# W2's 16-bit halves made in sweeps 0 and 1 and kept in memory, and block one-hots by one narrow 16-bit operation per pair

## The chip, the cores and the metric

One core of a Trainium2 chip. The time is the device time of one execution in microseconds (us), the median of several runs.

## What is computed

T=4096 tokens of D=256 features, a dense 4096x4096 adjacency of zeros and ones, E=8 experts.

```python
h = layernorm(x);   x = x + (adj @ (h @ W0 + b0)) / deg          # deg: column sums of adj
h = layernorm(x)
p = softmax(h @ Wg + bg); top 2 of 8, renormalised -> combine
x = x + sum_e combine_e * (gelu(h @ W1[e] + b1[e]) @ W2[e] + b2[e])
h = layernorm(x);   A = adj + I;  x = x + relu((d^-1/2 A d^-1/2 h) @ WL.T + bL)
x = x + a table step on the layernormed row (argmax of three groups of 16, a shift, two one-hots)
```

Products run on pairs of 16-bit numbers: a value v is kept as hi = fp16(v) and lo = fp16(v - hi), and three of the four products are summed.

## The kernel before, in words

The program has three blocks. A block begins only when all engines have ended the block before.

**Block 1, sweeps.** The first graph layer runs as NS=4 sweeps of 1024 columns. In a sweep SP loads 32 tiles of the adjacency (512 KB each) into a ring of 8; TensorE takes 8 products of 512 columns per tile (L914), ScalarE sums each tile for the degrees (add_degree, L802). A tile's buffer is free when both have used it. In sweep 0 the rows of x are normalised on the way: VectorE (rows, L484), then ScalarE casts the high half (high_row, L798; four rows ahead, then 4/3 rows per tile), then GpSimd takes the low half (split_row, L392). From tile 20 on TensorE transposes three rows per tile and multiplies them by the gate weights; each transposed row goes through take_transposed on VectorE (L545), with two buffers. At tile 21 it transposes W0, for which the row of b0 must have landed (L958); GpSimd issues that load behind its last split_row (L404), then two stores of zero rows, and waits for them (L408). Sweep 1 begins when VectorE has taken the gate sums (xg_taken, L559). In sweeps 1 to 3 the products of the sweep before leave by rows_out (L926), a row per tile from tile 4 on (from 20 in sweep 3).

**The weights.** The experts' weights are 32 units of 128x1024: u 0 to 15 of W1, 16 to 31 of W2. In memory of the core they take 16-bit halves for the whole of block 2. W1's 16 units are split in the sweeps at the tiles named by UNIT_AT (L277): SP loads a unit into one of two buffers (L311), ScalarE casts the high half behind add_degree (L810), VectorE makes the low half (split_unit, L492) at places written out by hand in its order (L573 to L595). W2's 16 units come behind sweep 3, during the last rows and the routing: SP loads them as f32 (load_middle_unit, L340; four late ones at L365), ScalarE makes the high half and a scaled copy (high_middle, L874), GpSimd subtracts (split_middle, L438); the four late ones are cast by ScalarE at the end of the block (L907) and subtracted by VectorE at the start of block 2 (split_late, L1235). Second-layer products wait for w2_parts (L1162).

**Late rows and routing.** GpSimd loads x a second time in pairs of tiles (load_x_again, L410) for the residual sums; the rows of tiles 16 to 31 are normalised on ScalarE (L825) and low halves made on GpSimd (L416) between the units of W2. VectorE ranks the tokens (L686 to L741) and then builds, in 16 batches of HOTS=4 pairs, one-hots of row and block; TensorE multiplies them (L1019) into the table of tokens. The block one-hot is two operations per batch, over 4x80 elements in f32 through a bank of PSUM (L756, L757).

**Block 2** gathers rows per expert slot (L1057), runs two layers on TensorE and adds the results to x_rows. **Block 3** is the second graph layer and the table step. The diff does not touch block 3.

Of the kernel before, what the change touches and what calls it, by code (L numbers as in the profile page):

```python
# [3 lines left out]
P = 128  # L4
# [67 lines left out]
def program(nc, x, adjT, W0, b0, Wg, bg, W1, b1t, W2, b2, WL, bL, identity, upper, out):  # L72

    ln_rows = nc.dram_tensor("ln_rows", [T + P, ROW], F32, kind="Internal").ap()
# [78 lines left out]

    stage = [Region(X_AT + 16384 + k * 4096, end)(f"stage{k}", [P, 1024], F32) for k in range(MIDDLE_RING)]
    late_stage = [Region(W_AT - 16384 + k * 4096, W_AT)(f"late_stage{k}", [P, 1024], F32) for k in range(UNITS - LATE_UNIT0)]
# [88 lines left out]
    same_blk = [pb[k][:, 0:HOTS * BLOCKS].rearrange("p (q b) -> p q b", b=BLOCKS) for k in (4, 3)]  # L244
# [36 lines left out]
    assert len(UNIT_AT) == W2_UNIT0 and NS == 4 and RING == G  # L281

    def unit_out(u, h):
        return w1_v[:, u, h, :, :]

    def unit_in(t):
        return unit_f[t][:, :].rearrange("p (h f) -> p h f", h=2)

    def middle_stage(u):
        return stage[(u - W2_UNIT0) % MIDDLE_RING]  # L290

# [15 lines left out]
    with nc.Block() as block:  # L307

        @block.sync
        def _(sp):  # L310
            def load_unit(u):  # L311
                sp.wait_ge(sem("unit_lo"), u + 1)
                sp.dma_start(unit_f[u % 2][:, :], W1_unit[u]).then_inc(sem(f"unit_loaded{u % 2}"), 16)
# [26 lines left out]
            def load_middle_unit(u):  # L340
                k = u - W2_UNIT0
                if k >= MIDDLE_RING:
                    sp.wait_ge(sem("middle_lo"), k - MIDDLE_RING + 1)
                sp.dma_start(middle_stage(u)[:, :].rearrange("p (f d) -> p f d", d=D), W2_u[k]
                             ).then_inc(sem(f"middle_loaded{k % MIDDLE_RING}"), 16)

            for k in range(4):
                sp.wait_ge(sem("adj_used"), 3 * NT + 29 + k + RING)
                sp.wait_ge(sem("deg_ready"), 3 * NT + 29 + k + RING)
                load_middle_unit(W2_UNIT0 + k)  # L350
            for g in range(2):
                store_x1(g)
            for k in range(4, 6):
                load_middle_unit(W2_UNIT0 + k)
            store_x1(2)
            for k in range(6, 8):
                load_middle_unit(W2_UNIT0 + k)
            store_rows(2)
            store_x1(3)
            for k in range(8, 10):  # L360
                load_middle_unit(W2_UNIT0 + k)
            store_rows(3)
            for k in range(2):
                sp.wait_ge(sem(f"early_stored{k}"), 16 * (NT // 8))
            for k in range(UNITS - LATE_UNIT0):  # L365
                sp.dma_start(late_stage[k][:, :].rearrange("p (f d) -> p f d", d=D), W2_u[LATE_UNIT0 - W2_UNIT0 + k]
                             ).then_inc(sem("late_loaded"), 16)
            for u in range(W2_UNIT0 + 10, LATE_UNIT0):
                load_middle_unit(u)
# [4 lines left out]
            sp.wait_ge(sem("late_stored"), 16 * 2)  # L374
# [3 lines left out]
        def _(pool):  # L378
# [17 lines left out]

            pool.sem_inc(sem("hid_lo_ready"), 2)
# [10 lines left out]
            pool.wait_ge(sem("spare_zeroed"), 32)  # L408

# [16 lines left out]
            pool.wait_ge(sem("unit_lo"), W2_UNIT0 + 2)  # L426
# [11 lines left out]
            def split_middle(u):  # L438
                pool.wait_ge(sem("middle_hi"), 2 * (u - W2_UNIT0) + 2)
                pool.tensor_tensor(experts[:, u, 1, :], middle_stage(u)[:, :], experts[:, u, 0, :], ALU.subtract  # L440
                                   ).then_inc(sem("middle_lo"), 1)

            for k in range(4):
                split_middle(W2_UNIT0 + k)
            for n in range(2 * G, 3 * G):
                low_row(n)
            for k in range(4, 6):
                split_middle(W2_UNIT0 + k)
            for n in range(3 * G, NT):
                low_row(n)  # L450
            for u in range(W2_UNIT0 + 6, LATE_UNIT0):
                split_middle(u)
# [4 lines left out]
        def _(v):  # L457
            v.sem_inc(sem("unit_lo"), 2)
# [114 lines left out]
            split_unit(0)  # L573
            split_unit(1)
            for n in range(NT):
# [8 lines left out]
            split_unit(3)  # L584
            take_numbers()

            for s in (1, 2):
                low_sums(s - 1)
                u = UNIT_AT[s, 4]
                split_unit(u)  # L590
                for k in range(OT):
                    take_rows((s - 1) * OT + k)
                    if k % 2:
                        split_unit(u + 1 + k // 2)
                split_unit(u + 5)  # L595
# [10 lines left out]
            def x_pair(n):  # L606
# [9 lines left out]
            def add_late_mean(n, bank):  # L616
                x_pair(n)
# [3 lines left out]
                v.scalar_tensor_tensor(out=agg[:, n, :], in0=bank[:, 0:D], scalar=rdeg[:, n:n + 1], in1=x_ring[:, n % G, :],  # L621
# [128 lines left out]
            for q in range(BATCHES):  # L750
# [5 lines left out]
                st.link(v.tensor_tensor(same_blk[i], over_pairs(count_ps[:, 0:BLOCKS]), over_columns(blk[:, k, :], n, BLOCKS), ALU.is_equal))  # L756
                v.tensor_tensor(blk_hot[i][:, :, :], same_blk[i], over_columns(val, n, BLOCKS), ALU.mult).then_inc(sem("hot_ready"), 1)  # L757
# [29 lines left out]
        def _(a):  # L787
# [13 lines left out]

            def add_degree(s, j):  # L802
# [4 lines left out]
                if (s, j) in UNIT_AT:  # L807
                    u = UNIT_AT[s, j]
                    a.wait_ge(sem(f"unit_loaded{u % 2}"), u // 2 * 16 + 16)
                    a.mul(unit_out(u, 0), unit_in(u % 2), WS).then_inc(sem("unit_hi"), 1)  # L810
# [63 lines left out]
            def high_middle(u):  # L874
                k = u - W2_UNIT0
                a.wait_ge(sem(f"middle_loaded{k % MIDDLE_RING}"), k // MIDDLE_RING * 16 + 16)
                if u == LATE_ROWS_UNIT:
# [761 lines left out]
```

## Time and profile before

| | us |
|---|---|
| median of 3 runs (lowest, highest) | 1075.37 (1074.89, 1077.36) |
| profiled execution | 1077.18 |
| its span, first to last instruction | 1075.2 |
| TensorE busy | 956.4 (89%) |
| VectorE busy | 559.4 (52%) |
| ScalarE busy | 404.4 (38%) |
| GpSimd busy | 360.0 (33%) |
| DMA | 200.00 MB, mean 186 GB/s |

An engine's share of the span is an average over stages with different limits, so the stages are read one by one below. Engines in the rows: PE is TensorE, PEld its weight loads, DVE VectorE, ACT ScalarE, POOL GpSimd, SP the engine that issues most transfers.

### The profile page before, as it was taken

To read this page: it belongs to the slowest core of one execution; us is meant where nothing else is said; L and a number is where in the kernel's file an instruction comes from. 1 tells how busy PE (TensorE), PEld (TensorE's weight loads), DVE (VectorE), ACT (ScalarE), POOL (GpSimd) and SP (SyncE) were. 2 spreads that over 40 slices of the span, in tenths; PEclk is the share of its full clock that TensorE was granted. 3 is DMA by queue.
4 is the path that set the end of the run, shared out by engine and by line. 5 is a ranking of instruction groups with operands and counts; after the bars stand their busy time and mean duration, and the time that the engine had idled before them with its cause. 6 is when DMAs were issued, how large, how long until landed. Compare 5 with 4: busy or idle time off the path is not lost. (4 is left out here: it accounts for less than half of the span.)

```text
span 1075.2 us, 22179 instructions
## 1 busy us (share of the span) xinstructions
PE 956.4 (89%) x6724; PEld 627.4 (58%) x6725; DVE 559.4 (52%) x1643; ACT 404.4 (38%) x826; POOL 360.0 (33%) x416
## 2 busy tenths in 40 slices
PE   4988999999922799999999999999819999999993
PEld 1444544444411689898989898898704454444541
DVE  6734113127598566565656565665436334161754
ACT  4863758676787233232323232323112101010111
POOL 3510000014575345454545455454425320110110
PEclk9999999999965799999999999999959999999997
DMA  9785898899786423232332323232259978876771
GB/s 346 307 293 186 287 328 319 312 345 371 257 278 183 156 41 55 45 54 45 50 50 45 54 43 56 40 55 44 46 161 393 406 254 298 291 240 189 231 254 35
DMA packets 91265, 200.00 MB, mean 186 GB/s; under 512 B 13328, under 2 KB 47120, under 8 KB 91088
## 3 DMA queue, kind: packets, MB, share of 16 engines
q1 hardware_dynamic: 69248, 164.17, 43.5%
q0 software_dynamic: 17792, 31.02, 14.6%
q10 hardware_dynamic: 4176, 4.19, 1.2%
q8 instruction: 26, 0.43, 0.2%
q14 instruction: 23, 0.19, 0.1%
HBM read 176.41 MB, written 22.94 MB: 185 GB/s over the span
## 5 line engine op out<-in xcount | busy, mean ns | idle before, releaser
L921 PE MATMUL bank<-adj_f,feat 128*128 128x512 f16 x1024 | 240.8, 390 | 17.4 <-DMA adj_f<-in_adjT 15.7
L1202 ACT ACTIVATE act_f<-bank,b_sb 128x256 f32<-128x256 f32 x304 | 127.6, 471 | 288.4 <-PE bank L1148 288.4
L1148 PE MATMUL bank<-rT,experts 128*128 128x256 f16 x1824 | 207.8, 275 | 0.9 <-DVE rT L1215 0.9
L1169 PE MATMUL bank<-experts,act_h 128*128 x1824 | 205.3, 273 | 1.4 <-DVE y_f L1247 1.4
L1148 PEld LDWEIGHTS bank<-rT,experts 128*128 x1824 | 179.5, 98 | 22.9 <-issue 1.2
L1169 PEld LDWEIGHTS bank<-experts,act_h 128*128 128x128 f16 x1824 | 176.8, 98 | 21.6 <-issue 1.7
L1064 POOL DMA_INDIRECT x_rows<-y,token x76 | 121.9, 1604 | 193.1 <-DVE y L1254 165.2
L921 PEld LDWEIGHTS bank<-adj_f,feat 128*128 128x128 f16 x1024 | 97.5, 96 | 144.4 <-issue 18.1
L1588 PE MATMUL bank<-adj_g,feat 128*128 128x512 f16 x768 | 179.7, 387 | 0.3 <-POOL feat L1393 0.3
L805 ACT ACTIVATE spent<-adj_f 128x1024 f16<-128x1024 f32 x128 | 135.1, 1055 | 33.5 <-DMA adj_f<-in_adjT 28.3
L1588 PEld LDWEIGHTS bank<-adj_g,feat 128*128 128x128 f16 x768 | 73.8, 96 | 94.1 <-issue 0.8
L1225 DVE TENSOR_TENSOR act_h<-act_f,act_h 128x512 f16<-128x512 f32 x152 | 105.3, 693 | 5.2
L1247 DVE SCALAR_TENSOR_TENSOR y_f<-bank,b_all 128x256 f32<-128x256 f32 x76 | 28.7, 419 | 112.6 <-PE bank L1169 112.6
L1223 DVE CAST act_h<-act_f 128x512 f16<-128x512 f32 x152 | 65.3, 429 | 39.3 <-ACT act_f L1202 39.0
L1588 PE MATMUL bank<-adj_early,feat 128*128 128x512 f16 x256 | 61.8, 398 | 25.3 <-POOL feat L1393 25.3
L1059 POOL DMA_INDIRECT rows<-ln_rows,token x72 | 76.4, 1061 | 22.1 <-issue 21.8
L414 POOL DMA_DIRECT2D x_ring<-in_x x16 | 11.6, 725 | 178.7 <-DVE experts L494 160.7
L1588 PEld LDWEIGHTS bank<-adj_early,feat 128*128 128x128 f16 x256 | 25.1, 98 | 60.4 <-issue 28.6
L494 DVE SCALAR_TENSOR_TENSOR experts<-unit_f,experts 128x1024 f16<-128x1024 f32 x16 | 20.0, 1252 | 76.0 <-ACT experts L810 76.0
L1449 DVE SCALAR_TENSOR_TENSOR agg_lo<-bank,agg_hi 128x512 f16<-128x512 f32 x16 | 10.0, 684 | 85.2 <-ACT agg_hi L1550 85.2
L1550 ACT ACTIVATE agg_hi<-bank 128x512 f16<-128x512 f32 x16 | 8.4, 600 | 98.4 <-PE bank L1588 98.4
L177 ACT ACTIVATE std<-ve 128x8 f32<-128x8 f32 x10 | 2.1, 209 | 103.2 <-DVE ve L1437 103.2
(258 smaller groups left out, 910.0 us busy)
## 6 DMA issues: line engine op xcount, KB each, us to landing
adj_f<-in_adjT SPq DMA_DIRECT2D x128, 512.0 KB, 6.7
adj_g<-in_adjT SPq DMA_DIRECT2D x72, 512.0 KB, 6.0
adj_early<-in_adjT SPq DMA_DIRECT2D x24, 512.0 KB, 6.6
adj_g<-in_adjT SPq DMA_DIRECT2D x48, 256.0 KB, 3.1
unit_f<-in_W SPq DMA_DIRECT2D x16, 512.0 KB, 7.3
stage<-in_W SPq DMA_DIRECT2D x12, 512.0 KB, 7.0
x_ring<-in_x POOLq DMA_DIRECT2D x16, 256.0 KB, 7.6
x_rows<-agg SPq DMA_DIRECT2D x4, 1024.0 KB, 9.6
```

The lines of the kernel that those rows point to most:

```text
L494: v.scalar_tensor_tensor(out=unit_out(u, 1), in0=unit_in(u % 2), scalar=WS, in1=unit_out(u, 0), op0=ALU.mult, op1=ALU.subtract).then_inc(s ...
L805: a.activation(spent[:, :], adj_f[j % RING][:, :], ACT.Copy, accum_out=degp[:, s, j:j + 1]).then_inc(sem("deg_ready"), 1)
L921: last = pe.matmul(mine(s)[ib * DC + c][:, :], feat0[:, j, h, c * P:(c + 1) * P], adj_0[j % RING][:, ib * HALF_SWEEP:(ib + 1) * HALF_SWEEP ...
L1059: pool.indirect_dma_start(rows[i][:, r, :], None, ln_rows[:, :], bass.IndirectOffsetOnAxis(ap=indices[:, at + r:at + r + 1], axis=0)).then ...
L1064: pool.indirect_dma_start(x_rows[:, :], bass.IndirectOffsetOnAxis(ap=token[i][:, r:r + 1], axis=0), y[i][:, r, :], None, compute_op=ALU.ad ...
L1148: last = pe.matmul(pb[2 + q][:, k * SLOT:(k + 1) * SLOT], w1_part(e * DC + (f // FQ * W2_UNIT0 + c), wh)[:, (f % FQ) * P:(f % FQ + 1) * P] ...
L1169: last = pe.matmul(pb[6 + r][:, 0:D], act_h[i][:, ah, f, r * P:(r + 1) * P], experts[:, ds(e * DC + (W2_UNIT0 + f // UH), 1), wh, (f % UH) ...
L1202: last = a.activation(act_f[q][:, k, :], pb[2 + q][:, k * SLOT:(k + 1) * SLOT], ACT.Gelu, bias=b1_sb[:, ds(e * FC + (2 * q + k), 1)], scal ...
L1223: v.tensor_copy(hi, act_f[q][:, :, :]).then_inc(sem("act_hi_ready"), 1)
L1225: v.tensor_tensor(act_h[i][:, 1, 2 * q:2 * q + 2, :], act_f[q][:, :, :], hi, ALU.subtract).then_inc(sem("act_h_ready"), 1)
L1247: last = v.scalar_tensor_tensor(out=y_f[:, r, :], in0=pb[6 + r][:, 0:D], scalar=1.0 / WS, in1=b2_all[:, ds(e, 1), :].rearrange("p a d -> p ...
L1588: last = pe.matmul(mine(s)[ib * DC + c][:, :], feat[:, j, h, c * P:(c + 1) * P], adj_1[b][:, ib * HALF_SWEEP:(ib + 1) * HALF_SWEEP], start ...
```

## The change

- *Units.* All 32 units are now split in sweeps 0 to 2, W2's first (q 0 to 15), 11, 11 and 10 per sweep, in a new order of tiles. Their loads are issued by GpSimd into a ring of four (the last six units of W1 into two buffers). In sweep 0 the first four loads follow GpSimd's splits of rows 28 to 31.
- *Parking.* The halves of a W2 unit are made in one of two buffers of 16-bit numbers and stored by GpSimd to a tensor in HBM (w2_split); ScalarE may cast unit q only when unit q-2 is stored. Behind sweep 3 SP loads the halves back, two units per transfer, in eight transfers.
- *Gone:* the f32 loads, casts and splits of W2 behind sweep 3 and at the start of block 2, and the waits for w2_parts. The adjacency tiles at the start of block 2 no longer wait for them.
- *x.* The second load of x goes for tiles 16 to 31: the sum takes the x that still lies in agg.
- *One-hots.* The block one-hot is one operation per pair: is_equal and mult with two scalars per partition, 80 numbers of 16 bits from SBUF to SBUF; TensorE waits per pair.

```diff
     UNIT_AT = {}
-    for s, at in ((0, range(5, 30, 8)), (1, range(4, 30, 5)), (2, range(4, 30, 5))):
+    for s, at in ((0, (18, 20, 21, 23, 24, 25, 27, 28, 29, 30, 31)), (1, range(1, 32, 3)), (2, range(1, 30, 3))):
...
@@ sync
-                    if (s, j) in UNIT_AT:
-                        load_unit(UNIT_AT[s, j])
...
+            def load_w2(u, units):
+                k = u - W2_UNIT0
+                sp.dma_start(experts[:, u:u + units, :, :], w2_split[k:k + units, :, :, :].rearrange("u p h f -> p u h f")
+                             ).then_inc(sem("w2_loaded"), 16)
+
+            store_x1(0)
+            store_x1(1)
+            sp.wait_ge(sem("adj_used"), NS * NT + RING)
+            sp.wait_ge(sem("deg_ready"), NS * NT + RING)
             for k in range(4):
+                load_w2(W2_UNIT0 + 2 * k, 2)
+            store_x1(2)
+            store_rows(2)
+            for k in range(6, 8):
+                load_w2(W2_UNIT0 + 2 * k, 2)
+            store_x1(3)
+            store_rows(3)
+            sp.wait_ge(sem("late_stored"), 16 * 2)
+            for k in range(4, 6):
+                load_w2(W2_UNIT0 + 2 * k, 2)
...
@@ gpsimd
+            def load_unit(q):
+                if UNIT_RING <= q < RINGED:
+                    pool.wait_ge(sem("unit_lo"), q - UNIT_RING + 1)
...
+            def park(q):
+                pool.wait_ge(sem("unit_lo"), q + 1)
+                pool.dma_start(w2_split[q, :, :, :], parked[q % 2][:, :, :]).then_inc(sem(f"parked{q % 2}"), 16)
+
             for n in range(NT):
                 split_row(n)
+                if n >= NT - UNIT_RING:
+                    load_unit(n - (NT - UNIT_RING))
...
             pool.wait_ge(sem("spare_zeroed"), 32)
+            for q in range(UNITS):
+                if q < W2_UNITS:
+                    park(q)
+                if q + UNIT_RING < UNITS:
+                    load_unit(q + UNIT_RING)
...
-                    load_x_again(G + n // 2)
...
@@ vector
-            split_unit(0)
-            split_unit(1)
+            SPLIT_BEHIND = {2: 0, 4: 1, 6: 2, 11: 3, 14: 4, 17: 5, 22: 6, 25: 7, 28: 8, 30: 9, 31: 10}
             for n in range(NT):
                 take_transposed(n)
...
-                if n == 18:
-                    split_unit(2)
+                if n in SPLIT_BEHIND:
+                    split_unit(SPLIT_BEHIND[n])
...
-                st.link(v.tensor_tensor(same_blk[i], over_pairs(count_ps[:, 0:BLOCKS]), over_columns(blk[:, k, :], n, BLOCKS), ALU.is_equal))
-                v.tensor_tensor(blk_hot[i][:, :, :], same_blk[i], over_columns(val, n, BLOCKS), ALU.mult).then_inc(sem("hot_ready"), 1)
+                for m in range(HOTS):
+                    v.tensor_scalar(blk_hot[i][:, m, :], count16[:, 0:BLOCKS], blk[:, k, n + m:n + m + 1], val[:, n + m:n + m + 1],
+                                    ALU.is_equal, ALU.mult).then_inc(sem("hot_ready"), 1)
...
@@ scalar
+            def high_unit(q):
+                a.wait_ge(sem(unit_sem(q)), unit_loads(q))
+                if 2 <= q < W2_UNITS:
+                    a.wait_ge(sem(f"parked{q % 2}"), q // 2 * 16)
...
+                a.mul(unit_out(q, 0), unit_in(q), WS).then_inc(sem("unit_hi"), 1)
...
-            for u in range(W2_UNIT0 + 8, LATE_UNIT0):
-                high_middle(u)
-            a.wait_ge(sem("middle_lo"), LATE_UNIT0 - W2_UNIT0)
-            a.wait_ge(sem("late_loaded"), 16 * (UNITS - LATE_UNIT0))
-            for k in range(UNITS - LATE_UNIT0):
-                a.mul(experts[:, LATE_UNIT0 + k, 0, :], late_stage[k][:, :], WS).then_inc(sem("late_hi"), 1)
...
@@ block 2
-            sp.wait_ge(sem("w2_parts"), UNITS - W2_UNIT0)
...
-                pe.wait_ge(sem("w2_parts"), e * 2 + 2)
...
-            v.sem_inc(sem("w2_parts"), LATE_UNIT0 - W2_UNIT0)
-            for k in range(UNITS - LATE_UNIT0):
-                split_late(k)
```

## Rows read from the trace of the kernel before

**Rows 1.** Windows: us, busy us (count) of five engines, TensorE's clock, DMA share, GB/s.

```profile
162.00:225.00 63.00, 63.00 (x304) 28.96 (x303) 13.18 (x26) 44.42 (x74) 2.91 (x4) 1.00 0.89 315
302.00:348.00 46.00, 8.38 (x68) 4.49 (x68) 41.82 (x117) 38.34 (x58) 31.35 (x26) 0.50 0.73 215
358.00:794.00 436.00, 417.63 (x3944) 374.51 (x3943) 253.26 (x530) 127.64 (x304) 210.16 (x190) 0.98 0.30 51
```

**Rows 2.** Timeline of TensorE in sweep 0: start, us, operation, idle before and its releaser.

```profile
62.23 0.66 PE L962 MATMUL bank<-ident,w_f 128*128 128x128 f32 x4 [2.39 <-DMA w_f<-in_b]
...
68.42 1.97 PE L921 MATMUL bank<-adj_f,feat 128*128 128x512 f16 x8
...
99.16 2.21 PE L921 MATMUL bank<-adj_f,feat 128*128 128x512 f16 x9 [1.66 <-DVE xg L559]
```

**Rows 3.** Timeline of ScalarE in sweep 0: a unit cast, and tiles 17 and 18.

```profile
42.29 1.04 ACT L810 ACTIVATE experts<-unit_f 128x1024 f16<-128x1024 f32 x1
...
50.12 1.05 ACT L805 ACTIVATE spent<-adj_f 128x1024 f16<-128x1024 f32 x1
...
51.47 1.05 ACT L805 ACTIVATE spent<-adj_f 128x1024 f16<-128x1024 f32 x1
```

**Rows 4.** Timeline of GpSimd in sweep 0: row splits, then b0 and zero rows.

```profile
49.99 2.33 POOL L394 TENSOR_TENSOR feat<-xn_ring,feat 128x255 f16<-128x255 f32 x3 [0.67 <-ACT feat L800]
...
56.41 0.68 POOL L404 DMA_DIRECT2D w_f<-in_b  x1
...
57.66 0.54 POOL L407 DMA_DIRECT2D x_rows<-zrow  x1
```

**Rows 5.** Transfers, median us to landing: three from 50 to 66 us; two of the whole span.

```profile
adj_f<-in_adjT SPq DMA_DIRECT2D x8, 512.0 KB, 9.1
...
x_rows<-zrow POOLq DMA_DIRECT2D x1, 128.0 KB, 6.7
w_f<-in_b POOLq DMA_DIRECT2D x1, 1.0 KB, 5.8
...
out<-made POOLq DMA_DIRECT2D x1, 512.0 KB, 3.4
...
DMA to landing us min/median/max: 3.3/7.3/11.9
```

The last row is of the 16 loads of unit_f, 512 KB each.

**Rows 6.** Timeline of VectorE in sweep 0: the split of a unit.

```profile
80.62 1.22 DVE L494 SCALAR_TENSOR_TENSOR experts<-unit_f,experts 128x1024 f16<-128x1024 f32 x1
```

**Rows 7.** Timeline of VectorE: the last batch of one-hots and what follows.

```profile
343.16 0.49 DVE L757 TENSOR_TENSOR blk_hot<-bank,val 128x320 f16<-128x320 f32 x1
343.57 0.68 DVE L754 TENSOR_TENSOR row_hot<-bank,row 128x512 f16<-128x512 f32 x1
344.16 0.49 DVE L756 TENSOR_TENSOR bank<-bank,blk 128x320 f32<-128x320 f32 x1
344.69 0.49 DVE L757 TENSOR_TENSOR blk_hot<-bank,val 128x320 f16<-128x320 f32 x1
345.72 0.25 DVE L779 TENSOR_SCALAR bank<-bank 128x80 f32<-128x80 f32 x1 [0.54 <-PE bank L1023]
```

**Rows 8.** Timeline of VectorE: operations with two pointer scalars, and with none.

```profile
247.47 2.67 DVE L651 TENSOR_SCALAR xn<-agg,mv,r 128x256 f32<-128x256 f32 x8
...
893.24 2.07 DVE L1474 TENSOR_SCALAR z<-x_sb,mv,rstd 128x112 f32<-128x112 f32 x8
...
315.61 0.30 DVE L733 TENSOR_SCALAR bank<-bank 128x32 int32<-128x32 int32 x2
```

**Rows 9.** Timelines around the seam between routing and experts.

```profile
346.64 0.16 DVE L784 TENSOR_SCALAR tokens<-spare 128x8 int32<-128x8 f32 x1
...
344.18 3.89 ACT L908 ACTIVATE experts<-late_stage 128x1024 f16<-128x1024 f32 x4 [2.43 <-POOL experts L440]
...
350.05 1.82 POOL L1059 DMA_INDIRECT rows<-ln_rows,first_tokens  x1 [0.57 <-POOL first_tokens L1080]
...
354.36 0.96 POOL L1059 DMA_INDIRECT rows<-ln_rows,first_tokens  x1 [0.30 <-issue]
```

More of the change, by code:

```diff
@@ L152, in w1_part @@
         return w1_flat[:, ds(half * 2 + h, 1), :].rearrange("p a f -> p (a f)")
-    stage = [Region(X_AT + 16384 + k * 4096, end)(f"stage{k}", [P, 1024], F32) for k in range(MIDDLE_RING)]
-    late_stage = [Region(W_AT - 16384 + k * 4096, W_AT)(f"late_stage{k}", [P, 1024], F32) for k in range(UNITS - LATE_UNIT0)]
+    unit_ring = [Region(at, X_AT)(f"unit_ring{k}", [P, 1024], F32)
+                 for k, at in enumerate(W_AT + row * 1024 for row in (8, 12, 40, 44))]
+    parked = [Region(W_AT + row * 1024, X_AT)(f"parked{k}", [P, 2, 1024], F16) for k, row in enumerate((28, 60))]
     LATE_AT = W_AT - 16384
@@ L277, in program, with w1_unit_of, unit_buffer, unit_sem @@
     UNIT_AT = {}
-    for s, at in ((0, range(5, 30, 8)), (1, range(4, 30, 5)), (2, range(4, 30, 5))):
+    for s, at in ((0, (18, 20, 21, 23, 24, 25, 27, 28, 29, 30, 31)), (1, range(1, 32, 3)), (2, range(1, 30, 3))):
         for j in at:
             UNIT_AT[s, j] = len(UNIT_AT)
[L281 to L290, printed above, removed]
+    RINGED_W1 = (0, 1, 2, 3, 8, 9, 10, 11, 12, 13)
+    LAST_W1 = (4, 5, 6, 7, 14, 15)
+    RINGED = W2_UNITS + len(RINGED_W1)
+    assert len(UNIT_AT) == UNITS == RINGED + len(LAST_W1) and NS == 4 and RING == G
+    def w1_unit_of(q):
+        return (RINGED_W1 + LAST_W1)[q - W2_UNITS]
+    def unit_buffer(q):
+        return unit_ring[q % UNIT_RING] if q < RINGED else unit_f[(q - RINGED) % 2]
+    def unit_sem(q):
+        return f"unit_loaded{q % UNIT_RING}" if q < RINGED else f"last_unit_loaded{(q - RINGED) % 2}"
+    def unit_loads(q):
+        return (q // UNIT_RING if q < RINGED else (q - RINGED) // 2) * 16 + 16
+    def unit_out(q, h):
+        return parked[q % 2][:, h, :] if q < W2_UNITS else w1_v[:, w1_unit_of(q), h, :, :]
+    def unit_in(q):
+        return unit_buffer(q)[:, :] if q < W2_UNITS else unit_buffer(q)[:, :].rearrange("p (h f) -> p h f", h=2)
     def place(n):
@@ L435, in _ @@
                     store_pair(n - 1)
-                    load_x_again(G + n // 2)
[L438 to L445, printed above, removed]
-                low_row(n)
[L447 to L452, printed above, removed]
+            for n in range(2 * G, NT):
+                low_row(n)
             for k in range(2):
@@ L588, in _ @@
                 low_sums(s - 1)
-                u = UNIT_AT[s, 4]
-                split_unit(u)
+                first = UNIT_AT[s, 1]
+                split_unit(first)
                 for k in range(OT):
                     take_rows((s - 1) * OT + k)
-                    if k % 2:
-                        split_unit(u + 1 + k // 2)
-                split_unit(u + 5)
+                    if k % 3 == 1:
+                        split_unit(first + 1 + k // 3)
+                for q in range(first + 4, min(first + 11, UNITS)):
+                    split_unit(q)
             st = Steps(v, sem("v_norm1"))
@@ L800, in high_row @@
                 a.copy(feat0[:, n, 0, 0:LAST], xn_ring[:, n % XN_RING, 0:LAST]).then_inc(sem("hid_hi_ready"), 1)
+            def high_unit(q):
+                a.wait_ge(sem(unit_sem(q)), unit_loads(q))
+                if 2 <= q < W2_UNITS:
+                    a.wait_ge(sem(f"parked{q % 2}"), q // 2 * 16)
+                if q >= RINGED:
+                    a.wait_ge(sem("unit_lo"), RINGED)
+                    for k in range(2):
+                        a.wait_ge(sem(f"parked{k}"), W2_UNITS // 2 * 16)
+                a.mul(unit_out(q, 0), unit_in(q), WS).then_inc(sem("unit_hi"), 1)
             def add_degree(s, j):
@@ L872, in _ @@
             high_sums(3)
[L874 to L877, printed above, removed]
-                    a.wait_ge(sem("late_stored"), 16 * 2)
-                a.mul(experts[:, u, 0, :], middle_stage(u)[:, :], WS).then_inc(sem("middle_hi"), 1)
-                a.mul(middle_stage(u)[:, :], middle_stage(u)[:, :], WS).then_inc(sem("middle_hi"), 1)
-            for k in range(2):
-                high_middle(W2_UNIT0 + k)
             for n in range(3 * G, NT):
@@ L1233, in next_rows @@
                               ).then_inc(sem("gates_taken"), 1)
-            def split_late(k):
-                v.wait_ge(sem("late_hi"), k + 1)
-                v.scalar_tensor_tensor(out=experts[:, LATE_UNIT0 + k, 1, :], in0=late_stage[k][:, :], scalar=WS,
-                                       in1=experts[:, LATE_UNIT0 + k, 0, :], op0=ALU.mult, op1=ALU.subtract
-                                       ).then_inc(sem("w2_parts"), 1)
             def take_y(s, i):
```

78 lines of the change are left out of this document (18 added, 60 removed).

## The prediction

> **What bounds the kernel now.** I read the stages first, in the windows [rows 1]: in sweep 2 (162 to 225 us; sweep 1 looks the same) TensorE is busy for the whole time and the DMA engines for 0.89 of it; in the routing stage (302 to 348) VectorE is busy 41.8 of 46 us and TensorE 8.4; from 358 to 794 TensorE has the experts to itself again. So a transfer or a cast hides in the sweeps as long as TensorE is never made to wait, and in routing only VectorE's chain counts. Then the order of work at the end of sweep 0, where the diff puts the most [rows 2 to 4]; the landing times [rows 5]; the split and one one-hot batch on VectorE [rows 6, 7]; what an operation of the new form costs [rows 8]; and the seam between routing and experts [rows 9].
>
> In sweep 0 the reader is to see that TensorE, ScalarE, VectorE and GpSimd are tied. TensorE waits for the row of b0 until 62.23, starts tile 23 at 68.42, and starts sweep 1 at 99.16 after 1.66 idle, so its last product ended at 97.5; VectorE's L559 releases it [rows 2]. Each queue is in order, and transposed rows pass through VectorE's take_transposed.
>
> **Sweep 0, step by step.** Removed: ScalarE's unit casts at tiles 5 and 13 (1.04 us each) [rows 3]; ScalarE ends tile 18 at 50.5 instead of 52.5 [rows 3]. SP no longer stands at its unit loads in this sweep; tiles come a little earlier, which nobody waits for.
> 1. *Unit 0.* Its load is now issued by GpSimd behind the split of row 28 (52.3 before [rows 4], now 50.4), and ScalarE wants it right behind tile 18. A load of this size landed in 3.3 at the least and 7.3 in the median; 512 KB from GpSimd's queue, alone, in 3.4 [rows 5]. With one tile in flight beside it I take 5: 55.4, cast done 56.4. ScalarE has stood still for 5 us; that alone costs nothing, since it is far ahead of TensorE (tile 18 done at 52.5, TensorE's tile 23 at 68.4).
> 2. *b0.* Queued behind the standing ScalarE are the casts of rows 29 to 31, behind these GpSimd's splits (2.33 for three, 0.78 each) and unit loads (issue 0.7, as that of b0 [rows 4]), and behind these the load of b0. A tile with a row's cast takes 1.35 (50.12 to 51.47 [rows 3]): 57.8. Row 30 is cast 0.3 later, and two splits, two issues and the small copy follow: b0 is issued at 61.2, not 56.4. It lands 5.8 later as now [rows 5]: 67.0. TensorE's wait at tile 21 grows by 4.8.
> 3. *Unit 2.* It may be written only when unit 0's halves are stored. That store stands behind GpSimd's wait for the zeroed rows: issued 1.2 after b0, landing 6.7 later [rows 4, 5], so 69.1. Store 5, cast 1.04, split 1.22 [rows 6]: 76.4. That split stands in VectorE's queue between transposed rows 6 and 7, and TensorE needs row 7 before tile 23: start 77.1 instead of 68.4. The loss is now 8.7.
> 4. *Units 4 to 10.* With two parking buffers, two units take a store, a cast and a split: 5+1.04+1.22 and 0.3 of hand-overs, 7.6. Four such steps from 76.4 end at 106.8. TensorE's own path ends at 77.1+29.1=106.2 (68.42 to 97.5 [rows 2]), so both chains bind in turn; places in VectorE's queue where one waits for the other add 1 to 2. Then x's gates, 2 us as now: sweep 1 starts at about 110, **11 us late**.
>
> The landing time rules this sum. At 3.4 for all of it the same steps give unit 2 split at 70.3, tile 23 at 71.3 and +3.4 in all; at 8, unit 2 split at 84, four steps of 10.6 and +29. Between these I draw lines: 4 gives +6, 6.5 gives +20. I take 5, nearer the low end, because tiles are consumed at 3.2 us apiece there and a standing ScalarE stops their loads. Nothing later wins the time back: the sweeps behind are TensorE's.
>
> **Sweeps 1 to 3.** Sweep 2 takes ten units instead of six: 2.1 MB more in 63 us, 33 GB/s on 315. 0.89 of DMA time becomes 0.98 [rows 1]: 0, at most +3, since a tile is asked for eight tiles (16 us) ahead and even the crowded ones landed in 9.1 [rows 5]. Sweep 1 takes eleven, five of them parked, 5.2 MB more; its first tiles are slowed by the row products. Casts and splits lie beside TensorE. GpSimd's queue now holds 32 unit loads and 16 parks, some 0.7 each, with nothing of sweeps 1 and 2 behind them but the first x loads, which move to just behind the last unit, still before the ScalarE tiles that their user waits for: 0. The eight x loads of sweep 3 and their GpSimd issues go, 2 MB; no engine waited for them on the path: 0.
>
> **Routing.** A batch is 0.60 for the row one-hots, then 0.53+0.41=0.93 for the two block operations (343.57, 344.16, 344.69, and the same spacing back to 343.16) [rows 7]. Four operations with two pointer scalars each replace them. The nearest rows have that form in f32: eight of 256 elements in 2.67, eight of 112 in 2.07 [rows 8]. That is 0.334 and 0.259 apiece (a little too much, the last one's tail is in it), so 0.52 ns per element on 0.20 fixed. 80 elements: 0.24 in f32, and no type gets under the fixed part. I take 0.22, four are 0.88: 0.05 less, in 16 batches **-0.8**. Bounds: -2.1 at 0.20, +2.4 if 80 elements cost twice as much each as in these rows and the fixed part stays (0.27 after the tail). A short operation without pointers comes every 0.11 (two in 0.30 [rows 8]); that is the rival below.
>
> The Trainium skill (VectorE: DVE Perf Modes, the section on the TRN2 errata) gives an SBUF operation 58 cycles plus its elements over the mode's 4, which would be 81 ns here, 0.33 per batch, and -9.7 in all. The same section says that the fixed part is paid per instruction and asks for tiles of 512 elements and more, which speaks against four of 80. The f32 rows with pointers lie far above its figure; no row here shows the 16-bit form.
>
> The last batch ends with one product behind it instead of four, and VectorE's wait of 0.54 there shortens [rows 7]: -0.2. W2's 24 ScalarE casts and copies, 12 GpSimd and 4 VectorE splits leave this part; all lie beside VectorE's chain but the last four casts, which end at 348.07, when VectorE has been done since 346.80 [rows 9]. The next block begins after both: **-1.0**. SP's 8 MB of halves replace 8 MB of f32; the pair held for the late rows waits for their store, which now can leave earlier, since 12 ScalarE operations of a us each are gone from in front of it. Hidden.
>
> **The seam.** Beside VectorE's four splits a row gather takes 1.82, without them 0.96 [rows 9]; two gathers stand before the first expert: up to -1.8. Against it, the adjacency tiles (2 MB) are now requested at once, beside b2 and these gathers. I take **-0.8**, bounds -1.8 and +1. The wait dropped from second_layer lies in a sequencer that runs ahead of a busy TensorE: 0.
>
> **Sum.** +11-0.8-0.2-1.0-0.8=+8.2. Against the profiled execution's 1077.18 that is 1085.4; it lay 1.8 above the median of 1075.37, so the median becomes **1083.6**.
>
> **Rivals.**
> - *Landings at their shortest* (3.4 throughout). For: 3.3 and 3.4 were seen; while ScalarE stands, no tiles are requested. Against: up to three unit loads go out together. +3.4-2.8: 1076.0. Chance 0.15.
> - *DMA runs full.* Each unit brings a load and a store, and W2's rows come in 1 KB pieces; landings of 7 (tiles at 50 to 66 took 9.1 [rows 5]) give +23 on the line from 5 to 8, sweep 2 up to +3: about 1098. Against: the stall throttles itself. Chance 0.12.
> - *The narrow operation is cheap*, the side of faster. Place: the 16 batches; price 0.11 instead of 0.22, so 0.44 against 0.93, -7.8 instead of -0.8. With my sweep 0 that is 1076.6; it decides once sweep 0 loses less than 9.8, and at landings of 4 (+6) gives 1071.6. For: the short rows; against: both rows with pointers. By the Trainium skill's figure (same section as above) it would be 2 us faster still. Chance 0.15.
> - *The one-hots don't get faster*, the change not doing what it says: 1084.4, or 1086.7 at 0.27 an operation; it lies inside the forecast's range and chance.
>
> **Numbers.** Forecast 0.58, rivals 0.15, 0.12, 0.15. Measurements of this kernel tell apart about 0.2%, 2.2 us. Faster: 0.03 from short landings and 0.08 from cheap operations, 0.11. Same: 0.09 and 0.05, 0.14. Slower: the rest, 0.75. The forecast's own range is landings of 4 to 6.5, +6 to +20, with the other terms at -5.5 to +0.6: 1076 to 1096. The range takes most of the short landings in: 1075 to 1096.
>
> **What would show it.** Right: ScalarE idle for 4 to 6 us behind tile 18, released by a unit load; b0 landing near 67; VectorE idle at the split of unit 2 and TensorE at the rows behind it; sweep 1 starting near 110; batches of 1.4 to 1.5 us with the four operations 0.2 apart; gathers near 1.0. Wrong: sweep 1 starting before 104, or operations under 0.15 apart. An idle TensorE in the middle of sweep 1 or 2 would mean that the DMA engines ran full.

## The result

The changed kernel took 1103.51 us in the median (1102.71 to 1103.87) beside 1076.36 us of the kernel before: ratio 1.0249, interval 1.0223 to 1.0275. One further execution, at a granted clock of 0.815 instead of 0.941, took 1211.17 us and is left out. The kernel is slower by 27 us. The forecast was 1083.6, 8.2 slower, with a range of 1075 to 1096: the sign was right, the size was not.

The profiled execution took 1103.51 us, span 1101.6 (before 1077.18 and 1075.2). Where the two traces part, stretch by stretch:

| stretch | forecast | measured |
|---|---|---|
| start of sweep 1 (99.16, after 123.68) | +11 | +24.5 |
| first tiles of sweep 1 | 0 | +2.2 |
| sweeps 2 and 3, late rows to the first one-hot | 0 | +0.4 |
| 16 batches of one-hots | -0.8 | -1.4 |
| last batch and the start of block 2 | -1.2 | -1.2 |
| from there to the first expert product | -0.8 | +2.0 |
| the rest | 0 | -0.1 |
| sum | +8.2 | +26.4 |

The rest is -1.0 in the first slots of the experts and +0.9 in the table step at the very end. The second shows in some kernels below (experiments 5, 6 and 8) and not in others (3, 4, 7, 9 and 10), with the same code there; I take it for scatter.

### The profile page after: what moved, and what is told of

It is laid out like the page before. It is cut to its first block and busy times, and to the rows that moved or that the text cites. A ratio compares the mean times of both kernels' runs of the same rounds, so it can differ in the third digit from the quotient of the medians.

```text
span 1101.6 us, 22191 instructions
## 1 busy us (share of the span) xinstructions
PE 968.7 (88%) x6724; PEld 631.9 (57%) x6725; DVE 575.5 (52%) x1687; ACT 390.7 (35%) x814; POOL 356.2 (32%) x444
## 5 line engine op out<-in xcount | busy, mean ns | idle before, releaser
L901 PE MATMUL bank<-adj_f,feat 128*128 128x512 f16 x1024 | 244.9, 395 | 20.8 <-DMA adj_f<-in_adjT 15.0
L1042 POOL DMA_INDIRECT x_rows<-y,token x76 | 121.9, 1604 | 192.9 <-DVE y L1225 166.3
L1424 DVE SCALAR_TENSOR_TENSOR proj<-bank,dinv_y,bL_all 128x256 f32<-128x256 f32 x32 | 15.5, 484 | 41.4 <-PE bank L184 41.3
L1346 POOL TENSOR_TENSOR adj_g<-adj_g,grow 128x128 f32<-128x128 f32 x24 | 11.1, 461 | 78.3 <-DMA adj_g<-in_adjT 78.3
```

What stands on the lines that cost most here:

```text
L901: last = pe.matmul(mine(s)[ib * DC + c][:, :], feat0[:, j, h, c * P:(c + 1) * P], adj_0[j % RING][:, ib * HALF_SWEEP:(ib + 1) * HALF_SWEEP ...
L1042: pool.indirect_dma_start(x_rows[:, :], bass.IndirectOffsetOnAxis(ap=token[i][:, r:r + 1], axis=0), y[i][:, r, :], None, compute_op=ALU.ad ...
```

## The profile after

The windows of the changed kernel, with the columns of [rows 1]; the first five cover the end of sweep 0 and the start of sweep 1, the last three answer to those rows:

```profile
45.00:57.00 12.00, 11.70 (x64) 5.27 (x63) 6.23 (x15) 5.75 (x13) 4.42 (x6) 1.00 0.88 289
57.00:76.00 19.00, 5.16 (x46) 3.30 (x44) 2.98 (x6) 6.14 (x11) 7.97 (x12) 0.67 0.66 217
76.00:99.00 23.00, 17.16 (x166) 9.45 (x165) 13.07 (x24) 12.02 (x19) 6.46 (x10) 0.95 0.94 324
99.00:124.00 25.00, 15.49 (x137) 8.57 (x136) 11.95 (x28) 12.45 (x20) 6.45 (x10) 0.77 0.96 330
124.00:128.00 4.00, 4.00 (x11) 1.37 (x10) 3.71 (x14) 3.91 (x7) 0.00 (x0) 0.50 0.67 244
...
189.00:252.00 63.00, 63.00 (x304) 28.75 (x303) 18.96 (x31) 47.54 (x78) 6.57 (x11) 1.00 0.91 344
329.00:374.00 45.00, 15.27 (x68) 6.92 (x68) 41.14 (x148) 16.20 (x33) 10.88 (x17) 0.51 0.59 193
385.00:820.00 435.00, 416.29 (x3942) 373.22 (x3940) 252.98 (x531) 127.58 (x305) 210.46 (x191) 0.98 0.29 47
```

and one window of the kernel before, for the first of them:

```profile
45.00:57.00 12.00, 12.00 (x60) 5.30 (x58) 9.85 (x23) 10.07 (x24) 7.39 (x11) 1.00 0.40 135
```

From 57 to 124 TensorE is busy for 38 of 67 us. Sweep 2 is as it was, with 0.91 of DMA time instead of 0.89. From 45 to 57 the DMA engines are now busy for 0.88 instead of 0.40 of the time. And from 124 to 128 the granted clock is 0.50, the 1.2 GHz level.

The timeline of TensorE in the changed kernel, which answers to [rows 2]:

```profile
73.01 1.12 PE L942 MATMUL bank<-ident,w_f 128*128 128x128 f32 x4 [13.84 <-DMA w_f<-in_b]
...
80.79 0.26 PE L925 MATMUL bank<-wgx,xT 128*128 128x16 f16 x4 [1.25 <-DVE xT L550]
80.90 1.97 PE L901 MATMUL bank<-adj_f,feat 128*128 128x512 f16 x8
...
96.69 0.26 PE L925 MATMUL bank<-wgx,xT 128*128 128x16 f16 x4 [3.03 <-DVE xT L550]
...
123.68 8.63 PE L901 MATMUL bank<-adj_f,feat 128*128 128x512 f16 x28 [5.81 <-DVE xg L560]
```

ScalarE, where it answers to [rows 3], and GpSimd, for [rows 4]:

```profile
58.26 1.06 ACT L807 ACTIVATE parked<-unit_ring 128x1024 f16<-128x1024 f32 x1 [7.51 <-DMA unit_ring<-in_W]
...
69.56 1.06 ACT L807 ACTIVATE parked<-unit_ring 128x1024 f16<-128x1024 f32 x1 [7.24 <-DMA unit_ring<-in_W]
...
78.08 1.06 ACT L807 ACTIVATE parked<-unit_ring 128x1024 f16<-128x1024 f32 x1 [6.43 <-DMA w_split<-parked]
```

```profile
50.40 0.90 POOL L400 DMA_DIRECT2D unit_ring<-in_W  x1
...
64.76 0.55 POOL L415 DMA_DIRECT2D w_f<-in_b  x1
...
73.73 0.54 POOL L404 DMA_DIRECT2D w_split<-parked  x1 [7.32 <-DMA x_rows<-zrow]
```

ScalarE stands at three units in turn, and what ends its wait is first a load, then a load, then a store. The last waits of VectorE in sweep 0 are at the splits of units 8, 9 and 10, in front of x's gates:

```profile
111.64 1.23 DVE L495 SCALAR_TENSOR_TENSOR parked<-unit_ring,parked 128x1024 f16<-128x1024 f32 x1 [3.64 <-ACT parked L807]
...
115.98 1.23 DVE L495 SCALAR_TENSOR_TENSOR parked<-unit_ring,parked 128x1024 f16<-128x1024 f32 x1 [2.46 <-ACT parked L807]
...
120.63 1.22 DVE L495 SCALAR_TENSOR_TENSOR parked<-unit_ring,parked 128x1024 f16<-128x1024 f32 x1 [3.09 <-ACT parked L807]
```

Transfers issued from 76 to 120 us, median to landing, beside the 5 us that I had taken:

```profile
adj_f<-in_adjT SPq DMA_DIRECT2D x10, 512.0 KB, 6.7
w_split<-parked POOLq DMA_DIRECT2D x9, 512.0 KB, 6.3
unit_ring<-in_W POOLq DMA_DIRECT2D x9, 512.0 KB, 8.8
```

What ScalarE waited for from 76 to 124, in all, times, longest. Each of the nine casts (units 2 to 10) waited for a store:

```profile
ACT parked L807 <- DMA w_split<-parked: 27.6, 9, 6.4
```

SP's request for tile 22, after and before:

```profile
45.20 0.33 SPq L327 DMA_DIRECT2D adj_f<-in_adjT  x1
```

```profile
54.02 0.38 SPq L319 DMA_DIRECT2D adj_f<-in_adjT  x1
```

A batch of one-hots on VectorE, for [rows 7] (four operations are grouped as x4):

```profile
367.95 0.68 DVE L750 TENSOR_TENSOR row_hot<-bank,row 128x512 f16<-128x512 f32 x1
368.56 0.93 DVE L753 TENSOR_SCALAR blk_hot<-count,blk,val 128x80 f16<-128x80 f16 x4
369.39 0.68 DVE L750 TENSOR_TENSOR row_hot<-bank,row 128x512 f16<-128x512 f32 x1
...
371.26 0.25 DVE L776 TENSOR_SCALAR bank<-bank 128x80 f32<-128x80 f32 x1 [0.34 <-PE bank L1002]
```

367.95 to 369.39 is 1.44 per batch (1.53 before), 0.21 per operation, and the wait at the end is 0.34 instead of 0.54. The seam, for [rows 9], first GpSimd and then TensorE:

```profile
374.55 1.06 POOL L1037 DMA_INDIRECT rows<-ln_rows,first_tokens  x1 [0.59 <-POOL first_tokens L1058]
375.93 0.98 POOL L1037 DMA_INDIRECT rows<-ln_rows,first_tokens  x1 [0.31 <-issue]
```

```profile
382.45 1.03 PE L1107 MATMUL bank<-ident,rows 128*128 128x128 f16 x8 [11.23 <-DMA rows<-ln_rows,first_tokens]
384.39 1.88 PE L1126 MATMUL bank<-rT,experts 128*128 128x256 f16 x8 [0.91 <-DVE rT L1192]
```

The gathers are issued in 1.0 instead of 1.8 us, as forecast, but the rows that they bring reach TensorE 5.5 us behind the second one's issue (376.91 to 382.45).

## The experiments

The kernels below are in three groups: each part of the change alone, each suspected wait of sweep 0 alone, and all repairs together. "Before" is 1076.6 to 1078.2 us in the medians beside them; the ratios are to it.

**1. The one-hots alone, on the kernel before.** The edit is the one-hot part of the diff, nothing else.

> The kernel before with the one-hots of the change alone. Theory (a pointer form costs a fixed 0.2 us): in the changed kernel a batch took 1.44 us (367.95 to 369.39) where the kernel before took 1.53, so 16 batches give -1.4, and the last batch has one product behind it: the routing chain ends 1.5 to 1.7 us earlier. The end of block 1 is then set by ScalarE's last casts of W2, which ended 1.3 us behind VectorE before, so little of it reaches the end: total 0 to -0.5 us. Rival: the batches got faster only because ScalarE and GpSimd had less to do beside them; then a batch takes 1.5 or more here and nothing is gained. The narrow operation as cheap as 0.11 us would give batches of 1.05.

Measured: 1088.47 us, ratio 1.0098 (1.0081 to 1.0115), by which it is 10.5 us slower. Both theories fall. The last one-hot ended 12.6 us later than before. VectorE and GpSimd at the same moment of this kernel:

```profile
331.17 0.68 DVE L753 TENSOR_TENSOR row_hot<-bank,row 128x512 f16<-128x512 f32 x1
331.77 4.60 DVE L756 TENSOR_SCALAR blk_hot<-count,blk,val 128x80 f16<-128x80 f16 x4
336.28 0.68 DVE L753 TENSOR_TENSOR row_hot<-bank,row 128x512 f16<-128x512 f32 x1
...
332.09 4.24 POOL L439 TENSOR_TENSOR experts<-stage,experts 128x1024 f16<-128x1024 f32 x2 [2.32 <-ACT stage L880]
```

Four operations take 4.60 us where they take 0.93 in the changed kernel, and they come free when GpSimd's two splits of W2 end (336.33). Of the 64 operations 13 took longer than 0.4 us, up to 2.23, together 14.3 us more than 0.3 each, and every one of the 13 ended 0.04 us behind the end of a GpSimd operation. None of the 51 short ones lay inside a GpSimd operation. The row one-hot, read from PSUM, took its 0.68 throughout.

**2. The same with the block numbers read from PSUM.**

```diff
-                    v.tensor_scalar(blk_hot[i][:, m, :], count16[:, 0:BLOCKS], blk[...], val[...],
+                    v.tensor_scalar(blk_hot[i][:, m, :], count_ps[:, 0:BLOCKS], blk[...], val[...],
```

> The kernel before with the one-hots of the change, but the 80 block numbers are read as f32 from the bank of PSUM instead of 16-bit from SBUF; still one operation per pair. With the one-hots of the change on the kernel before, the chain of routing ended 12.9 us later: 16 or so of the 64 operations took 0.7 or 1.4 to 2.2 us where the rest took 0.3, and they end with GpSimd's operations (2.12 us splits of W2, 0.7 row splits) that ran at the same time. Theory 'lock': the 16-bit form from SBUF to SBUF needs something that GpSimd's operations hold, and the form from PSUM does not; no operation takes over 0.5 us, a batch takes 1.5 to 1.7, the last one-hot ends within 2 us of the kernel before (345.2), the total is within 2 us of before. Rival: it is the write of 16-bit rows or the pointers that are blocked; then the long operations stay and the total is 8 to 12 us above before.

Measured: 1077.46 us, ratio 1.0005 (0.9996 to 1.0015). No operation took over 0.36 us, though 29 of the 64 lay wholly inside an operation of GpSimd (its splits took 4.21 for two):

```profile
342.34 1.16 DVE L756 TENSOR_SCALAR blk_hot<-bank,blk,val 128x80 f16<-128x80 f32 x4
343.42 0.68 DVE L753 TENSOR_TENSOR row_hot<-bank,row 128x512 f16<-128x512 f32 x1
```

A batch is 1.67 us (1.53 before), 0.27 per operation. So the 16-bit form from SBUF to SBUF is shut out while GpSimd works, and the f32 form from PSUM is not; the pointers and the 16-bit result are the same in both. Which of the two differences counts, the place of the block numbers or their width, no run separates. The Trainium skill states this as a rule (SBUF — State Buffer, the section "Who interferes with whom"): VectorE in a two-port mode and GpSimd take a shared pair of ports by turns, and whoever comes second "fully blocks". These two traces agree, with 2.2 us for a GpSimd operation of 2.12, though they don't name the mode of an operation. In the changed kernel GpSimd has no splits of W2 behind sweep 3, its last row split ends at 343.82, and the first one-hot starts at 343.94: GpSimd is idle through all 16 batches, and so they take 1.44.

**3. Earlier unit loads.** `if n in (20, 22, 24, 26)` in place of `n >= 28` behind split_row.

> The changed kernel with the first four unit loads issued by GpSimd behind the splits of rows 20, 22, 24 and 26 instead of 28 to 31. Theory 'order of the queues': units 0 and 1 have landed when ScalarE comes to them, it doesn't stand at tiles 18 and 20, rows 29 to 31 are cast by 57, b0 is issued near 57.5 and lands by 65, and tile 22 starts near 66 instead of 75.7; unit 2 still waits for the zeroed rows and the first store (near 66 + 6), so tile 23 starts near 74 instead of 80.9, and behind it the two parking buffers pace the rest as now: sweep 1 starts near 117 instead of 123.7, total 1097. Rival 'traffic': the tail of sweep 0 is bounded by the bytes, 11 loads and 11 stores of 512 KB beside 14 tiles, whatever their order; then the loads only collide with x and the tiles earlier, and sweep 1 starts at 122 or later, total within 2 us of 1103.7.

Measured: 1090.42 us, ratio 1.0116; tile 22 at 61.5, tile 23 at 69.5, sweep 1 at 112.6, 11.1 us earlier than in the changed kernel. That is more than the expected 117: the second unit too had landed in time, and the first two stores went out 1.3 us apart. Traffic alone would have left it at 122.

**4. Eight parking buffers.**

```diff
-    parked = [... enumerate((28, 60))]
+    parked = [... enumerate((16, 20, 24, 28, 48, 52, 56, 60))]
```

> The changed kernel with eight parking buffers instead of two (in memory of W1's units 8 to 15, which is written only later). Theory 'order': up to tile 22 (75.7) nothing changes; from there ScalarE never waits for a store, only for the loads, so the splits stay ahead of the transposed rows; TensorE takes its 31 us from tile 23 to sweep 1: sweep 1 near 110 to 112 instead of 123.7, total near 1091. Rival 'traffic': the same 22 transfers run through the DMA engines, loads landing in 9 us and more take the place of the stores as the wait; sweep 1 at 120 or later, total 1100 or more.

Measured: 1095.20 us, ratio 1.0162; tile 22 at 75.1, sweep 1 at 116.7. Between the theories: 7 us earlier, not 12. The stores are no longer waited for, but the loads behind them land later. Issued from 76 to 117 us:

```profile
w_split<-parked POOLq DMA_DIRECT2D x10, 512.0 KB, 10.2
unit_ring<-in_W POOLq DMA_DIRECT2D x10, 512.0 KB, 11.8
```

**5. b0 first.** GpSimd issues the load of b0 in front of the first unit load.

> The changed kernel with b0's load issued by GpSimd in front of the first unit load, at about 50.5 instead of 64.8. It then lands near 57 and TensorE reaches tile 22 near 64 as in the kernel before, 11 us earlier than in the changed one. Theory 'chain of waits': nothing is gained, because tile 23 needs transposed row 7, which stands in VectorE's queue behind the split of unit 2 (79.2 in the changed kernel), and that waits for unit 0's store behind the zeroed rows: tile 23 starts at 79.5 to 80.9, sweep 1 within 1.5 us of 123.7, total 1102 to 1104. Rival 'b0 alone': the late row of b0 is what cost the first 11 us: sweep 1 at 113, total 1093.

Measured: 1101.07 us, ratio 1.0220; tile 22 at 61.10 instead of 75.73, tile 23 at 80.04 instead of 80.90, sweep 1 at 123.1. The timeline of TensorE in this kernel:

```profile
61.10 1.97 PE L903 MATMUL bank<-adj_f,feat 128*128 128x512 f16 x8
...
71.36 0.27 PE L927 MATMUL bank<-wgx,xT 128*128 128x16 f16 x4 [8.07 <-DVE xT L552]
...
79.91 0.27 PE L927 MATMUL bank<-wgx,xT 128*128 128x16 f16 x4 [7.30 <-DVE xT L552]
```

and VectorE at the splits of units 1 and 2:

```profile
69.74 1.23 DVE L497 SCALAR_TENSOR_TENSOR parked<-unit_ring,parked 128x1024 f16<-128x1024 f32 x1 [8.82 <-ACT parked L809]
...
78.29 1.23 DVE L497 SCALAR_TENSOR_TENSOR parked<-unit_ring,parked 128x1024 f16<-128x1024 f32 x1 [6.66 <-ACT parked L809]
```

14.6 us were won at tile 22 and 13.8 of them were gone at tile 23. The wait of 13.84 us for b0 in the changed kernel cost under 1 us by itself at tile 23: behind it stood rows held by the splits of units 1 and 2. The medians differ by 2.4 us, of which the two traces show 0.9; the rest is open.

**6. The last splits behind x's gates.** Units 8, 9 and 10 leave SPLIT_BEHIND and are split behind take_numbers.

> The changed kernel with the splits of units 8, 9 and 10 moved on VectorE from between transposed rows 28 to 31 to behind x's gates and the numbers. Theory 'order': sweep 1 waits for x's gates, and these for the splits in front of them; without them TensorE goes from tile 31 (about 111 instead of 113.7) to sweep 1 at about 115 instead of 123.7, and the total is 8 us less, 1095.7. Rival 'traffic': sweep 1 then finds its tiles late or the row products wait for sums that ScalarE casts behind unit 10 (120.5), and the time is lost again by tile 4 of sweep 1: total within 2 us of 1103.7.

Measured: 1100.36 us, ratio 1.0214. Sweep 1 started at 117.4, 6.3 us earlier (tile 31 did not move, against my expectation: unit 7 and the rows in front of it set it). Then 1.5 us went to the low sums, and TensorE waited for tiles, each a little (2.9 in all), until 24.2 of the former 26.7 us were back by tile 20; the DMA share from 136 to 189 is 1.03, which is full. Both theories hold, one behind the other, and 3 us remain in the medians. The traced execution took 1103.70, the others 1099.5 to 1100.7; its lead of 2.7 at the end of the sweeps was lost behind them.

**7. Earlier loads and eight buffers, then also the zeroed rows.** The second kernel moves GpSimd's wait for the zeroed rows behind all parks. It ran before the first, whose expectation therefore knows its 99.6.

> The changed kernel with earlier unit loads and eight parking buffers, but GpSimd still waits for the zeroed rows in front of the first park. With all three sweep 1 began at 99.6. Theory 'the wait only shifts the first stores and ring loads': the zeroed rows land near 61, the first park and the load of unit 4 are issued at 61 instead of 58, so the splits from unit 4 on are 3 us later: sweep 1 at 100 to 103, total 1080 to 1082. Rival 'the zeroed rows are what counts': sweep 1 at 107 or later.

> The changed kernel with the first unit loads behind the splits of rows 20, 22, 24, 26, eight parking buffers, and GpSimd's wait for the zeroed rows behind all parks. Earlier loads alone brought sweep 1 to 112.6, eight buffers alone to 116.7. Theory 'order': every wait of the new chain is gone, the splits keep pace with the transposed rows, tile 22 starts near 63 and sweep 1 near 102 to 104, total 1081 to 1083. Rival 'traffic': with eight buffers the stores and loads landed in 9 to 15 us instead of 6 to 9 (the DMA engines were full from 76 on), so the last units' loads still hold the splits behind rows 28 to 31: sweep 1 at 107 or later, total 1086 or more.

Measured: 1081.07 us, ratio 1.0045, sweep 1 at 101.9; and 1079.31, ratio 1.0020, sweep 1 at 99.6 (99.16 before). The windows of the second:

```profile
57.00:76.00 19.00, 15.27 (x164) 8.94 (x163) 12.64 (x24) 10.76 (x19) 6.46 (x10) 1.00 1.03 386
76.00:99.00 23.00, 16.84 (x171) 9.95 (x169) 13.36 (x26) 11.88 (x18) 7.41 (x12) 1.00 1.02 399
99.00:110.00 11.00, 10.43 (x42) 4.28 (x43) 4.56 (x19) 10.54 (x19) 1.62 (x3) 0.85 1.03 397
```

The DMA engines are full without a gap and loads land in 11.8 us, and yet sweep 1 starts within 0.4 us of where it did before the change. The 24.5 us were order and not bytes: the same loads and stores are in sweep 0 here, but in the changed kernel TensorE, ScalarE and at times the DMA engines (0.66 from 57 to 76) stood while one transfer at a time was waited for.

**8. The seam.** SP waits for the first gathers before it asks for the early adjacency tiles.

```diff
+            for i in range(2):
+                sp.wait_ge(sem(f"rows_loaded{i}"), 16 * SR)
             for j in range(EARLY):
```

> The changed kernel with the four early adjacency tiles of block 2 requested only when the first four row gathers have landed. Theory: their 2 MB made the gathers land late (issue of the second pair's first transpose 5.5 us behind the gathers' issue instead of 1.9); without them the first layer-1 product starts 8.1 us behind the barrier instead of 11.7, and the total falls by 3.6 us to about 1100.1. Rival: the gathers are late for another reason (b2's load, the state of the clock, the table's read); then the first product stays at 11 to 12 us and the total within 1 us of 1103.7.

Measured: 1098.72 us, ratio 1.0196. From the first gather to the first expert product it took 6.14 us instead of 9.84, so 3.7 are won at the seam, and they are still won at the end (4.2 there, with 0.5 from before the seam):

```profile
378.26 1.03 PE L1109 MATMUL bank<-ident,rows 128*128 128x128 f16 x8 [7.53 <-DMA rows<-ln_rows,first_tokens]
380.20 3.17 PE L1128 MATMUL bank<-rT,experts 128*128 128x256 f16 x14 [0.91 <-DVE rT L1194]
```

**9. All four repairs, and the price of the one-hots in them.**

> The changed kernel with the first unit loads behind the splits of rows 20, 22, 24, 26, eight parking buffers, the wait for the zeroed rows behind all parks, and the early adjacency tiles of block 2 behind the first gathers. Without the last of these it stood at a ratio of 1.002 to the kernel before; the gate alone brought the first layer-1 product 4.2 us forward. Theory 'the parts add up': 4 us less than without the gate, ratio 0.998, 1075 us, below both kernels. Rival: at the seam the tiles of the adjacency are then missing when block 3 begins, or the routing's end is now bounded elsewhere; ratio 1.000 or more.

> The same as the kernel with all four repairs, but with the block one-hots of the kernel before (two operations per batch over a bank of PSUM), so that the one-hots alone are priced where no GpSimd work runs beside them. Theory: a batch is 1.53 instead of 1.44 us and the last product comes later: 1.4 to 1.7 us slower, ratio higher by 0.0014. Rival: these 1.5 us are hidden (ScalarE's or GpSimd's last rows, the loads of W2's halves or the store of the gates end last), so the ratio is the same.

Measured: 1074.63 us, ratio 0.9982 (0.9973 to 0.9991), and with the old one-hots 1076.37, ratio 1.0002 (0.9989 to 1.0015). From the first one-hot to the last the traces give 26.97 and 28.39 us: 1.42, or 0.09 in each of 16 batches. It reaches the end of the program; the two medians differ by 1.7. So even with all four repairs and the old one-hots the split in the sweeps has won nothing over the kernel before (1.0002); what the repaired kernel wins comes from the one-hots, which need an idle GpSimd.

**10. One unit fewer in sweep 0.**

```diff
-    ... (0, (18, 20, 21, 23, 24, 25, 27, 28, 29, 30, 31)), ... (2, range(1, 30, 3))):
+    ... (0, (18, 20, 21, 23, 24, 25, 27, 28, 29, 30)), ... (2, range(1, 32, 3))):
```

> All four repairs, and one unit moved from the end of sweep 0 to sweep 2's end (10, 11, 11 units), so that one split fewer stands in front of x's gates. In the kernel with three repairs the last split of sweep 0 began at 96.5 and sweep 1 at 99.6 with TensorE idle and its clock down for the first tile. Theory: sweep 1 begins 2 to 3 us earlier and the total is 2 to 3 us below the kernel with all four repairs, 1072 to 1073. Rival: the DMA engines are full from 45 to 162 (share 0.98 to 1.03), so the tiles of sweep 1 come later instead and nothing is gained.

Measured: 1070.19 us, ratio 0.9934 (0.9920 to 0.9948), the fastest of all, 4.4 us below the kernel with eleven. The start of sweep 1 with eleven units, and with ten:

```profile
100.66 7.61 PE L903 MATMUL bank<-adj_f,feat 128*128 128x512 f16 x21 [5.83 <-DVE xg L561]
```

```profile
96.48 10.81 PE L903 MATMUL bank<-adj_f,feat 128*128 128x512 f16 x40 [1.66 <-DVE xg L561]
```

Sweep 1 starts 4.2 us earlier, and by tile 2 the lead is 5.27 us; 2 to 3 were expected. Not all of it is the split that no longer stands in front of x's gates. The second kernel of experiment 7 and the one with the old one-hots have the same code there as the kernel with eleven, and they start sweep 1 at 99.6. TensorE's granted clock from 98 to 106 was 0.50 in the trace of eleven, 0.79 and 0.67 in those two, and 0.82 with ten units. Against those two the lead is 3.1 us at the start and 2.7 to 3.2 at tile 2. That much is the split's; the rest of the 4.4 between the medians stays open.

## Why the forecast was right and wrong

The step that failed is step 4, the chain of units 4 to 10 through two buffers, and with it the landing time of 5 us that all of sweep 0 was priced with. Two units took 10.4 us and not 7.6, so behind tile 23 the loss grew by 12.0 us where the forecast had 2.3, and sweep 1 started 24.5 us late and not 11. The other steps in turn:

- **What binds.** Right: the chain through ScalarE, VectorE and GpSimd at the end of sweep 0 decides, and sweeps 2 and 3 hide everything else; the DMA share in sweep 2 was 0.91 and not 0.98. Of the named signs, ScalarE idle behind tile 18 and b0 late were there. VectorE idle at unit 2 was hardly there: 0.19 us (79.17), since TensorE, held by b0, brought row 6 no earlier than 78.56. The two chains ended together.
- **Step 1, unit 0: mis-sized.** I took a landing of 5 us and it took 7.8 (50.40 to 58.24). The failed sentence is that tiles come earlier, "which nobody waits for": SP asked for tile 22 at 45.20 instead of 54.02, since it no longer stands at unit loads, and tiles 22 to 26 were in flight beside unit 0 (share 0.88 against 0.40). No run takes these tiles away, so this cause is argued and not shown. ScalarE stood for 7.5 us, not 5.
- **Step 2, b0: mis-sized.** Issued at 64.76, not 61.2, and landed 8.2 later, not 5.8, behind three unit loads: 72.96 instead of 67.0. But this loss was hidden in step 3 (experiment 5).
- **Step 3, unit 2: the path was right.** Zeroed rows landed at 73.45 (69.1), the split began at 79.17 and tile 23 at 80.90 (77.1): +12.5 instead of +8.7.
- **Step 4, units 4 to 10: mis-sized, the largest error.** The path was right. The four steps took from 80.4 to 121.9, 10.4 us each, not 7.6. Stores landed in 7.1 us on the mean of those that were waited for, which is 2.1 of the 2.8 per step, and most of the rest is unit 6, which waited 1.85 us for its place in VectorE's queue. Experiment 4 takes the wait for stores away, and 7.0 us of the loss go. My line for landings of 8 had four steps of 10.6 in it; I gave it to a rival.
- **The choice of 5.** I reasoned that a standing ScalarE stops the tiles and thins the traffic. In the trace it does so only once: from 59 to 61 nothing is moved, and then three unit loads go out within 3 us and take 8.5 to 8.9. From 76 to 124 the share is 0.94 to 0.96 while TensorE waits, since each split releases a store and a load at once, and the tiles of the ring follow. The rival "DMA runs full" (landings of 7, +23 in sweep 0, chance 0.12) is what came in sweep 0; its +3 in sweep 2 did not come. Its name misleads, though: full engines don't cost 23 us by themselves (experiment 7: share 1.02 to 1.03, loads landing in 11.8), long landings in a chain with two buffers do.
- **The start of sweep 1: missing.** TensorE had been idle for 5.81 us; the granted clock was 0.50 from 124 to 128, and the first tile took 3.6 us instead of 2.0. That is the +2.2, and no step of mine had it.
- **One-hots: right.** 0.21 per operation against the 0.22 taken; -1.4 against -0.8. The rival of 0.11 didn't come. The 81 ns of the Trainium skill (VectorE: DVE Perf Modes, the section on the TRN2 errata), an estimate from its table, didn't come either; the same section says that its row comes out too low. What I missed is that this price needs an idle GpSimd: on the kernel before, the same edit costs 10.5 us (experiment 1). The forecast added up the two parts of the change as if they didn't touch each other.
- **Last batch and barrier: right**, -1.2.
- **The seam: wrong side.** It cost +2.0 and not -0.8, outside its bounds of -1.8 and +1. The issue of the two gathers fell by 1.66 us, as said. But the adjacency tiles delayed the gathers' rows by 3.65 us (1.9 from issue to TensorE before, 5.5 after), and experiment 8 gives it back.

## What to carry to other kernels

When a cast is moved in front of a store that must land before the buffer is used again, price the chain as landing time times steps through the buffers, with the landing time of a crowded queue, and ask first how many buffers there are and what stands behind the wait in each queue. The longest wait of a timeline may be worth nothing: repair it alone, and see what is late next. Before a VectorE operation is made narrow and 16-bit, look what GpSimd does at that moment. And a transfer that nobody needs soon should not be requested beside one that everybody waits for.

## What the runs showed of the hardware

- A 16-bit VectorE operation from SBUF to SBUF of 0.3 us takes up to 2.23 us beside GpSimd's elementwise operations of 2.12 (experiment 1); read from PSUM as f32 it takes 0.35, also inside them (experiment 2).
- With 80 elements and two scalars per partition the 16-bit form comes every 0.21 us, the f32 form from PSUM every 0.27.
- Software-issued loads of 512 KB land in 11.8 us in the median with the DMA engines at 1.02 of their time (experiment 7), in 8.8 at 0.95 (the changed kernel), where the quickest of the kernel before took 3.3 [rows 5]. A load of 1 KB behind three of them took 8.2, and 5.3 in front of them (experiment 5).
- The same code in sweep 0 (experiments 7 and 9) started sweep 1 at 99.6 in two traces and at 100.7 in a third: about 1 us is not to be read from a single trace.
